# Where TensorE makes the products with the values in a slot of the local attention layers

## The chip, the cores and the metric

The kernel runs on one core of a Trainium2 chip. The metric is the device time of one launch in microseconds; less is better. Everything is computed in single precision.

## What is computed

The reference is a stack of four blocks on 4 sequences of 256 tokens of 128 features. Each block is a cross attention and a feed forward part, both gated. The change touches only the feed forward part of the first block. That one is itself a transformer of six layers with local attention:

```python
for i in range(DEPTH):                      # DEPTH = 6
    x = attn_layer(shift_tokens(x), Wqkv[i], q_scale[i], k_scale[i], Wo[i]) + x
    x = ffn_layer(shift_tokens(x), ln_g[i], ln_b[i], W1[i], b1[i], W2[i], b2[i]) + x
```

`attn_layer` makes queries, keys and values for 16 heads of 64 features, normalises queries and keys to length one, rotates them by tables, and lets each window of 32 queries look at its own 32 keys and the 32 before them, with a softmax over those 64. `ffn_layer` is a layer norm, a product with W1 (128 x 682), a split into a hidden half `a` and a gate half, `a * gelu(gate)`, and a product with W2.

## The kernel before, in words

Every engine (TensorE, VectorE, ScalarE, GpSimd and SyncE for the DMAs) has its own queue, written out by hand; semaphores hold them together. Before and after the local layers come other stages, which the change leaves alone. The local layers are `pe_local`, `act_local`, `dve_local`, `pool_local` and one for SyncE.

The work of the local layers is cut into 96 units: 6 layers x 4 sequences x 2 tiles of 128 tokens x 2 halves of 8 heads. `for slot in range(LOCAL_SLOTS)` runs over 108 slots, and a unit passes through several slots in a pipeline: in slot u its queries, keys and values are made (L616, L636, L625), in slot u + 2 queries (L645) and keys (L653) are turned, in slot u + 3 the scores are made (L675), in slot u + 5 the softmax weights are turned (L686) and multiplied with the values (L702), in slot u + 6 the output product is made (L717). "Turned" is a transpose by TensorE against the identity, four blocks of 128x128.

The feed forward part belongs to a sequence and layer, that is to four units, and its pieces hang on every fourth slot: the centring product of its layer norm (L234) and the variance product (L244) in one slot, two slots later the first gate products (L557, L558) and the third (L566), one slot later the hidden products (L574, L575 and, separately, the last one, L583), one slot later the product with W2 (L592). I call these, by what stands in them, the variance slot, the gate slot, the open slot, and again the variance slot of the next; the slot that has none is plain. In each cycle of four slots there is a variance slot, a plain slot, a gate slot and an open slot, in that order. (L557 and L558 stand ahead of L636 and so appear in the timeline at the end of the stretch that begins with the plain slot's scores.)

The buffers in PSUM are single: queries, keys, values, turned queries and keys (the bank TB), turned weights (PB) and feed forward (FB) have one bank each. So most products wait for the copy out of their bank. The waits that matter here:

- L702 waits for ScalarE's copy of the turned weights (L842), for the value windows that SyncE moves, and for the copy of the values (L804).
- L645 waits for ScalarE's copy of the turned keys (L820), L717 for the copy of the weighted values (L850).
- L244 waits for ScalarE's squares (L239, `ln_squared`).
- L566 waits for ScalarE's copies of both gate products (L866 and L867, `gate01_kept`), L574 for that of the third (L873).

ScalarE's own order in a slot is: squares of the queries (L790), exponentials (L835), the third gate's copy (L873), turned queries (L811), values (L804), squares of the keys (L797), turned weights (L842), gate copies (L866, L867), squares for the layer norm (L239), gelu with its two table loads (L880 to L882), turned keys (L820), weighted values (L850), norms (L826 to L830). VectorE's L953 adds the mask to the scores (`masked`), and L583 waits for it.

Of the kernel before, what the change touches and what calls it, by code (L numbers as in the profile page):

```python
# [195 lines left out]
UNITS = DEPTH * B * LAYER_UNITS  # L196
TURN, SCORE, SOFT, VALUE, OUT = 2, 3, 4, 5, 6
CENTRE, SQUARE, VAR, RSTD, NORM, SCALE = 10, 10, 10, 11, 11, 11
GATES, KEEP, GATE2, KEEP2, GELU, OPEN, MIX = 12, 12, 12, 13, 13, 13, 13
LAST, HIDE, MERGE, RENEW = 13, 14, 14, 15  # L200
# [12 lines left out]
def ended(slot, lag):  # L213
    lb, rest = divmod(slot - lag, LAYER_UNITS)
    return lb if rest == 0 and 0 <= lb < DEPTH * B else None
# [6 lines left out]
def home_of(lb):  # L222
    return lb // B + 1, lb % B
# [9 lines left out]
def pe_ln_centre(e, s, m, bank, src):  # L233
    e.matmul(bank[:, 0:N], m.centre, src, start=True, stop=True, skip_group_check=True).then_inc(s["ln_centred"], 1)  # L234
# [27 lines left out]
def pe_ln4(e, s, m, first, bufs):  # L262
    for b in range(B):
        pe_ln_var(e, s, m, first + b, ln_views(bufs[b]), m.bank[2 * b])
# [277 lines left out]
def pe_centre(e, s, m, lb):  # L542
    e.wait_ge(s["y_added"], 4 * lb + 4)
    if lb:
        e.wait_ge(s["a01_done"], lb)
    pe_ln_centre(e, s, m, m.bank[FB], m.zs[lb % B])
# [6 lines left out]
def pe_gates(e, s, m, lb):  # L553
    stage, b = home_of(lb)
    w1 = m.W(stage, "W1")
    e.wait_ge(s["xn_scaled"], lb + 1)
    e.matmul(m.bank[FB][:, 0:N], w1[:, FF:FF + P], m.xn[b], start=True, stop=True, skip_group_check=True)  # L557
    e.matmul(m.bank[FB][:, N:2 * N], w1[:, FF + P:FF + 2 * P], m.xn[b], start=True, stop=True,  # L558
             skip_group_check=True).then_inc(s["gate01_made"], 1)
# [19 lines left out]
def pe_last_hidden(e, s, m, lb, scored):  # L579
    stage, b = home_of(lb)  # L580
    rows = FFC[2][1]
    e.wait_ge(s["masked"], scored)
    e.matmul(m.bank[S1][0:rows, N:2 * N], m.W(stage, "W1")[:, 2 * P:FF], m.xn[b], start=True, stop=True,  # L583
             skip_group_check=True).then_inc(s["a2_made"], 1)
# [12 lines left out]
def windows_loaded(u):  # L597
    even, odd = (16 * 2 * n for n in (4, 5))
    return sum(odd if unit_of(v)[3] else even for v in range(u % 2, u + 1, 2))


def live(u):
    return 0 <= u < UNITS


def pe_query(e, s, m, u):
    lb, stage, b, t, half = unit_of(u)
    if t == 0 and half == 0:
        e.wait_ge(s["z_ready"], max(lb + 1, B))
        if b == 0 and stage % 2:  # L610
            e.wait_ge(s["slot1_loaded"], loaded(stage))
        if b == 0 and stage % 2 == 0:
            e.wait_ge(s["slot0_loaded"], loaded(stage))
    if u:
        e.wait_ge(s["q_products"], u)
    e.matmul(m.bank[QB], m.zs[b][:, t * P:(t + 1) * P], m.W(stage, "Wqkv")[:, half * BANK:(half + 1) * BANK], start=True,  # L616
             stop=True, skip_group_check=True).then_inc(s["q_made"], 1)


def pe_key(e, s, m, u):  # L620
    lb, stage, b, t, half = unit_of(u)
    at = INNER + half * BANK
    if u:
        e.wait_ge(s["k_products"], u)
    e.matmul(m.bank[KB], m.zs[b][:, t * P:(t + 1) * P], m.W(stage, "Wqkv")[:, at:at + BANK], start=True,  # L625
             stop=True, skip_group_check=True).then_inc(s["k_made"], 1)


def pe_value(e, s, m, u):
    lb, stage, b, t, half = unit_of(u)  # L630
    at = 2 * INNER + half * BANK
    if 0 < u <= VALUE:
        e.wait_ge(s["v_kept"], u)
    if u > VALUE:
        e.wait_ge(s["o_kept"], u - VALUE)
    e.matmul(m.bank[VB], m.zs[b][:, t * P:(t + 1) * P], m.W(stage, "Wqkv")[:, at:at + BANK], start=True,  # L636
             stop=True, skip_group_check=True).then_inc(s["v_made"], 1)


def pe_turn_query(e, s, m, u):  # L640
    e.wait_ge(s["q_rotated"], u + 1)
    if u:
        e.wait_ge(s["k_kept"], u)
    for r in range(UP):
        made = e.transpose(m.bank[TB][:, r * P:(r + 1) * P], m.rot_q[u % ROTS][:, r * P:(r + 1) * P], m.ident)  # L645
    made.then_inc(s["q_turned"], 1)


def pe_turn_key(e, s, m, u):
    e.wait_ge(s["k_rotated"], u + 1)  # L650
    e.wait_ge(s["q_kept"], u + 1)
    for r in range(UP):
        made = e.transpose(m.bank[TB][:, r * P:(r + 1) * P], m.rot_k[u % ROTS][:, r * P:(r + 1) * P], m.ident)  # L653
    made.then_inc(s["k_turned"], 1)
# [35 lines left out]
def pe_weighted(e, s, m, u):  # L690
    v, pT = m.v64[u % 6].rearrange("p (i k d) -> p i k d", i=4, k=UP), m.pT[u % 2]
    e.wait_ge(s["p_kept"], u + 1)
    e.wait_ge(s["v64_odd"] if u % 2 else s["v64_even"], windows_loaded(u))
    e.wait_ge(s["v_kept"], min(u + VALUE + 1, UNITS))
    for c in range(2):
        for i in range(4):
            for y in range(2):
                k = 2 * c + y
                at, to = k * P + i * WINDOW, c * P + i * WINDOW
                for x in range(2):  # L700
                    rows = slice(x * DH, (x + 1) * DH)
                    made = e.matmul(m.bank[PB if x else VB][y * DH:(y + 1) * DH, to:to + WINDOW], v[rows, i, k, :],  # L702
                                    pT[rows, at:at + WINDOW], start=True, stop=True, skip_group_check=True)
    made.then_inc(s["o_made"], 1)


def pe_out(e, s, m, u):
    lb, stage, b, t, half = unit_of(u)
    wo, oT = m.W(stage, "Wo"), m.oT[u % 2]
    e.wait_ge(s["o_kept"], u + 1)  # L710
    if u + OUT - SCORE > UNITS:
        e.wait_ge(s["y_added"], u)
    else:
        e.wait_ge(s["masked"], u + OUT - SCORE)
    for k in range(UP):
        c = half * UP + k
        made = e.matmul(m.bank[S0][:, N:N + P], wo[:, c * D:(c + 1) * D], oT[:, k * P:(k + 1) * P], start=(k == 0),  # L717
                        stop=(k == UP - 1), skip_group_check=True)
    made.then_inc(s["y_made"], 1)
# [10 lines left out]
def pe_local(e, s, m):  # L730
    e.wait_ge(s["x_done"], B)
    for b in range(B):
        pe_ln_centre(e, s, m, m.bank[2 * b], m.x[b])
    pe_ln4(e, s, m, B, m.ln_first)
    for slot in range(LOCAL_SLOTS):
        if live(slot):
            pe_query(e, s, m, slot)
        if live(slot - TURN):
            pe_turn_query(e, s, m, slot - TURN)
        if live(slot - OUT):  # L740
            pe_out(e, s, m, slot - OUT)
        if ended(slot, GATES) is not None:
            pe_gates(e, s, m, ended(slot, GATES))
        if live(slot):
            pe_value(e, s, m, slot)
            pe_key(e, s, m, slot)
        if ended(slot, CENTRE) is not None:
            pe_centre(e, s, m, ended(slot, CENTRE))
        if slot == UNITS + 1:
            e.wait_ge(s["k_products"], UNITS)  # L750
        if slot == UNITS + CENTRE - 4:
            pe_idle(e, m, KB, 2)
        if live(slot - VALUE):
            pe_turn_weights(e, s, m, slot - VALUE)
        if live(slot - SCORE):
            pe_scores(e, s, m, slot - SCORE)
        if live(slot - VALUE):
            pe_weighted(e, s, m, slot - VALUE)
        if ended(slot, VAR) is not None:
            pe_var(e, s, m, ended(slot, VAR))  # L760
        if slot == UNITS + VAR - 4:
            pe_idle(e, m, KB, 8)
        if ended(slot, OPEN) is not None:
            pe_hidden(e, s, m, ended(slot, OPEN))
        if ended(slot, LAST) is not None:
            pe_last_hidden(e, s, m, ended(slot, LAST), min(slot - SCORE + 1, UNITS))
        if slot == UNITS + GATE2 - 4:
            pe_idle(e, m, KB, 3)
        if ended(slot, GATE2) is not None:
            pe_last_gate(e, s, m, ended(slot, GATE2))  # L770
        if slot == UNITS + GATE2 - 4:
            pe_idle(e, m, KB, 2)
        if live(slot - TURN):
            pe_turn_key(e, s, m, slot - TURN)
        if UNITS < slot < UNITS + VALUE:
            pe_idle(e, m, KB, 4)
        if slot == UNITS + MERGE - 4:
            for b in range(B - 1):
                e.wait_ge(s["ffn_added"], b + 1)
                pe_ln_centre(e, s, m, m.bank[2 * b], m.x[b])  # L780
            pe_idle(e, m, KB, 3)
        if ended(slot, MERGE) is not None:
            pe_ffn_out(e, s, m, ended(slot, MERGE), min(slot - SCORE + 1, UNITS))
# [1405 lines left out]
```

## Time and profile before

| | us |
|---|---|
| median of 3 runs | 1386.46 |
| lowest and highest run | 1381.38, 1390.13 |
| the profiled execution | 1376.86 |
| its span | 1375.0 |
| TensorE busy | 1260.2 (92%) |
| VectorE busy | 975.7 (71%) |
| ScalarE busy | 933.4 (68%) |
| GpSimd busy | 741.9 (54%) |

The span runs from the first to the last instruction of the profiled execution; the run's own time is 1.9 us longer. All rows below are from this one execution. The local layers take from about 190 to 1055 us of it. A row of TensorE's products has two times: when the group starts, and how long it is busy, of which the end is modelled. How long a step holds TensorE's queue is therefore read from the start of one row to the start of the next.

### The profile page before, as it was taken

Reading aid. Unit: us, or ns where it says so; the run is one execution under the profiler, and the core shown is the slowest. Engines: PE = TensorE matmul, PEld = TensorE weight load, DVE = VectorE, ACT = ScalarE, POOL = GpSimd, SP = SyncE. Lnnn points to the kernel's source line nnn. Section 1 sums busy time; section 2 is a strip of 40 time slices with the busy share of each in tenths; the row PEclk is TensorE's granted clock in tenths of the full one; section 3 lists DMA queues with packets and bytes.
Section 4 is the critical chain, followed back from the end, with each engine's and each line's share of the span. In section 5 each row is a group of like instructions: output and inputs, shape, how many; then the busy total and the mean of one; then the engine's idle time right before and its main releaser. Section 6 shows DMA issues by size and latency. Waiting matters only on the chain. (4 is left out here: it accounts for less than half of the span.)

```text
span 1375.0 us, 45266 instructions
## 1 busy us (share of the span) xinstructions
PE 1260.2 (92%) x18136; PEld 910.2 (66%) x18136; DVE 975.7 (71%) x2481; ACT 933.4 (68%) x2297; POOL 741.9 (54%) x749
## 2 busy tenths in 40 slices
PE   6999977999999999999999999999887998998767
PEld 5777635676776776667766776667676767775444
DVE  3666657887888888888877888888834545554666
ACT  5777745676777777777776777777655656654771
POOL 3444447887878887788877877878720001003000
PEclk9999999999999999999999999999999999999799
DMA  4000032222225222522242225222302000000000
GB/s 198 1 2 1 1 114 69 68 62 55 62 62 143 60 63 60 142 59 63 65 139 54 63 61 143 58 61 66 92 3 100 0 1 28 1 0 1 1 1 16
DMA packets 68320, 76.97 MB, mean 56 GB/s; under 512 B 14864, under 2 KB 62992, under 8 KB 67600
## 3 DMA queue, kind: packets, MB, share of 16 engines
q1 hardware_dynamic: 68112, 74.07, 20.2%
q8 instruction: 145, 2.38, 0.8%
q14 instruction: 63, 0.52, 0.1%
HBM read 26.31 MB, written 0.52 MB: 20 GB/s over the span
## 5 line engine op out<-in xcount | busy, mean ns | idle before, releaser
L1072 POOL TENSOR_TENSOR arena<-arena,small 128x512 f32<-128x512 f32 x96 | 100.1, 1043 | 154.1 <-DVE small L955 154.1
L820 ACT ACTIVATE arena<-banks 128x512 f32<-128x512 f32 x96 | 57.4, 598 | 149.8 <-PE banks L653 149.5
L931 DVE TENSOR_TENSOR arena<-banks,rotary 128x512 f32<-128x512 f32 x192 | 131.6, 686 | 29.3 <-ACT arena L790 17.4
L1047 POOL TENSOR_TENSOR arena<-arena 128x512 f32<-128x512 f32 x96 | 122.6, 1277 | 38.2 <-DVE arena L933 38.2
L702 PE MATMUL banks<-arena 64*64 64x32 f32 x6144 | 113.5, 222 | 18.2 <-issue 11.1
L1052 POOL TENSOR_TENSOR arena<-arena 128x512 f32<-128x512 f32 x96 | 122.5, 1276 | 0.4 <-DVE arena L933 0.4
L702 PEld LDWEIGHTS banks<-arena 64*64 64x64 f32 x6144 | 101.2, 136 | 29.8 <-issue 11.6
L503 POOL TENSOR_TENSOR arena<-arena,small 128x512 f32<-128x512 f32 x64 | 66.5, 1040 | 88.2 <-DVE small L437 88.2
L616 PE MATMUL banks<-slot,z 128*128 128x512 f32 x192 | 101.5, 611 | 7.1 <-DVE arena L933 3.6
L717 PE MATMUL banks<-arena,slot 128*128 128x128 f32 x768 | 104.2, 279 | 0.2 <-DVE arena L953 0.2
L1059 POOL TENSOR_TENSOR arena<-arena,small 128x512 f32<-128x512 f32 x96 | 100.4, 1046 | 2.3 <-ACT small L830 2.3
L1078 POOL TENSOR_TENSOR arena<-arena,small 128x512 f32<-128x512 f32 x96 | 100.1, 1042 | 0.9 <-DVE small L963 0.9
L1066 POOL TENSOR_TENSOR arena<-arena,small 128x512 f32<-128x512 f32 x96 | 100.0, 1042 | 0.0
L636 PE MATMUL banks<-slot,z 128*128 128x512 f32 x192 | 98.6, 595 | 0.0
L625 PE MATMUL banks<-slot,z 128*128 128x512 f32 x192 | 98.1, 593 | 0.0
L717 PEld LDWEIGHTS banks<-arena,slot 128*128 128x128 f32 x768 | 93.6, 192 | 1.0 <-ACT arena L850 0.4
L645 PEld LDWEIGHTS banks<-constants,arena 128*128 128x128 f32 x384 | 43.1, 143 | 72.6 <-issue 71.7
L383 ACT ACTIVATE arena<-arena,small 128x256 f32<-128x256 f32 x128 | 63.7, 500 | 39.8 <-DVE small L466 39.8
L972 DVE TENSOR_TENSOR z<-z,banks 64x128 f32<-64x128 f32 x96 | 26.6, 277 | 90.3 <-PE banks L717 90.2
L675 PE MATMUL banks<-arena 64*32 64x64 f32 x6144 | 83.4, 225 | 1.0 <-issue 0.5
L686 PEld LDWEIGHTS banks<-constants,arena 128*128 128x128 f32 x384 | 47.7, 142 | 50.1 <-issue 30.8
L675 PEld LDWEIGHTS banks<-arena 64*32 64x32 f32 x6144 | 68.1, 106 | 18.5 <-issue 18.5
(310 smaller groups left out, 3371.2 us busy)
## 6 DMA issues: line engine op xcount, KB each, us to landing
arena<-arena SPq DMA_DIRECT2D x576, 64.0 KB, 2.0
slot<-in_pack_dram SPq DMA_DIRECT2D x28, 339.5 KB
arena<-arena SPq DMA_DIRECT2D x288, 32.0 KB, 1.8
slot<-in_pack_dram SPq DMA_DIRECT2D x2, 2713.5 KB
slot<-in_pack_dram SPq DMA_DIRECT2D x1, 3333.0 KB
slot<-in_pack_dram SPq DMA_DIRECT2D x1, 2316.5 KB
slot<-in_pack_dram SPq DMA_DIRECT2D x4, 337.0 KB
slot<-in_pack_dram SPq DMA_DIRECT2D x7, 158.0 KB
```

Source lines behind the costliest of these rows:

```text
L616: e.matmul(m.bank[QB], m.zs[b][:, t * P:(t + 1) * P], m.W(stage, "Wqkv")[:, half * BANK:(half + 1) * BANK], start=True, stop=True, skip_gr ...
L636: e.matmul(m.bank[VB], m.zs[b][:, t * P:(t + 1) * P], m.W(stage, "Wqkv")[:, at:at + BANK], start=True, stop=True, skip_group_check=True).t ...
L675: made = e.matmul(m.bank[S0 + z][i * WINDOW:(i + 1) * WINDOW, r * SPAN:(r + 1) * SPAN], qT[rows, r, i * WINDOW:(i + 1) * WINDOW], kT[rows, ...
L702: made = e.matmul(m.bank[PB if x else VB][y * DH:(y + 1) * DH, to:to + WINDOW], v[rows, i, k, :], pT[rows, at:at + WINDOW], start=True, st ...
L717: made = e.matmul(m.bank[S0][:, N:N + P], wo[:, c * D:(c + 1) * D], oT[:, k * P:(k + 1) * P], start=(k == 0), stop=(k == UP - 1), skip_gro ...
L931: e.tensor_tensor(rot, made, cos, ALU.mult)
L1047: e.tensor_tensor(m.rot_q[u % ROTS], m.rot_q[u % ROTS], m.sin_q[u % 2], ALU.add).then_inc(s["q_added"], 1)
L1052: e.tensor_tensor(m.rot_k[u % ROTS], m.rot_k[u % ROTS], m.sin_k[u % 2], ALU.add).then_inc(s["k_added"], 1)
L1059: e.tensor_tensor(q, q, stretch(m.local_small[u % 4][:, 0:UH], DH), ALU.mult).then_inc(s["q_rotated"], 1)
L1066: e.tensor_tensor(k, k, stretch(m.local_small[u % 4][:, UH:2 * UH], DH), ALU.mult).then_inc(s["k_rotated"], 1)
L1072: e.tensor_tensor(p, p, stretch(m.local_small[u % 4][:, 16:24], SPAN), ALU.subtract).then_inc(s["lowered"], 1)
L1078: e.tensor_tensor(p, p, stretch(m.local_small[u % 4][:, 32:40], SPAN), ALU.mult).then_inc(s["normalised"], 1)
```

## The change

In `pe_local`, two blocks move. The products with the values (`pe_weighted`, L702) stood right behind the scores; now they stand behind the variance product, the hidden products, the third gate product and the turned keys. The last hidden product (`pe_last_hidden`, L583) goes with them and stands behind them. No other engine's order changes, and the products and waits themselves are the same.

```diff
         if live(slot - SCORE):
             pe_scores(e, s, m, slot - SCORE)
-        if live(slot - VALUE):
-            pe_weighted(e, s, m, slot - VALUE)
         if ended(slot, VAR) is not None:
             pe_var(e, s, m, ended(slot, VAR))
...
         if ended(slot, OPEN) is not None:
             pe_hidden(e, s, m, ended(slot, OPEN))
-        if ended(slot, LAST) is not None:
-            pe_last_hidden(e, s, m, ended(slot, LAST), min(slot - SCORE + 1, UNITS))
...
         if live(slot - TURN):
             pe_turn_key(e, s, m, slot - TURN)
+        if live(slot - VALUE):
+            pe_weighted(e, s, m, slot - VALUE)
+        if ended(slot, LAST) is not None:
+            pe_last_hidden(e, s, m, ended(slot, LAST), min(slot - SCORE + 1, UNITS))
```

TensorE's queue from the scores of a gate slot on, before (L675 scores, L702 products with the values, L566 third gate product, L653 turned keys, L616 next queries):

```order
L675 MATMUL banks<-arena 32x64 [waits a2_done,masked,z_ready,y_added,k_kept]
L675 MATMUL banks<-arena 32x64 x31
L702 MATMUL banks<-arena 64x32 [waits v_kept,v64_odd,p_kept]
L702 MATMUL banks<-arena 64x32 x31
L566 MATMUL banks<-xn,slot 85x256 [waits gate01_kept]
L653 MATMUL banks<-constants,arena 128x128 [waits q_kept,k_rotated]
L653 MATMUL banks<-constants,arena 128x128 x3
L616 MATMUL banks<-slot,z 128x512 [waits q_products]
```

The same place in the changed kernel:

```order
L675 MATMUL banks<-arena 32x64 [waits a2_done,masked,z_ready,y_added,k_kept]
L675 MATMUL banks<-arena 32x64 x31
L566 MATMUL banks<-xn,slot 85x256 [waits gate01_kept]
L653 MATMUL banks<-constants,arena 128x128 [waits q_kept,k_rotated]
L653 MATMUL banks<-constants,arena 128x128 x3
L702 MATMUL banks<-arena 64x32 [waits v_kept,v64_odd,p_kept]
L702 MATMUL banks<-arena 64x32 x31
L616 MATMUL banks<-slot,z 128x512 [waits q_products]
```

L566, with its wait for `gate01_kept`, now stands directly behind the scores, and the turned keys and the products with the values are queued behind it.

In an open slot of the changed kernel TensorE's queue reads (L574, L575 and L583 are the hidden products):

```order
L675 MATMUL banks<-arena 32x64 x31
L574 MATMUL banks<-xn,slot 128x256 [waits gate2_kept]
L575 MATMUL banks<-xn,slot 128x256
L653 MATMUL banks<-constants,arena 128x128 [waits q_kept,k_rotated]
L653 MATMUL banks<-constants,arena 128x128 x3
L702 MATMUL banks<-arena 64x32 [waits v_kept,v64_even,p_kept]
L702 MATMUL banks<-arena 64x32 x31
L583 MATMUL banks<-xn,slot 85x256 [waits masked]
```

Before, L702 stood ahead of L574, and L583 ahead of L653.

## Rows read from the trace of the kernel before

**Rows 1.** The page, section 1: busy time, share of the span and instructions.

```profile
PE 1260.2 (92%) x18136; PEld 910.2 (66%) x18136; DVE 975.7 (71%) x2481; ACT 933.4 (68%) x2297; POOL 741.9 (54%) x749
```

**Rows 2.** Busy time by stretch: length, PE, PEld, DVE, ACT, POOL, PEclk, DMA.

```profile
742.00:775.50 33.50, 33.05 (x661) 23.98 (x667) 28.58 (x64) 25.52 (x56) 26.84 (x26) 1.00 0.26 61
719.00:731.00 12.00, 8.96 (x156) 6.17 (x155) 5.95 (x12) 6.52 (x16) 11.07 (x15) 0.86 0.21 50
```

**Rows 3.** TensorE's waits: line, releaser, us in total, times, longest.

```profile
PE banks L702 <- issue: 11.1, 13, 2.2
...
PE banks L702 <- ACT arena L842: 6.8, 21, 0.7
PE banks L645 <- ACT arena L820: 6.6, 18, 0.8
```

**Rows 4.** Timeline of a plain slot, TensorE: start, busy, line, operation.

```profile
750.24 0.60 PE L686 MATMUL banks<-constants,arena 128*128 128x128 f32 x4
750.77 0.86 PE L675 MATMUL banks<-arena 64*32 64x64 f32 x64
751.58 1.14 PE L702 MATMUL banks<-arena 64*64 64x32 f32 x64
752.64 0.66 PE L653 MATMUL banks<-constants,arena 128*128 128x128 f32 x4
753.13 1.02 PE L616 MATMUL banks<-slot,z 128*128 128x512 f32 x2
754.08 0.63 PE L645 MATMUL banks<-constants,arena 128*128 128x128 f32 x4
754.54 1.09 PE L717 MATMUL banks<-arena,slot 128*128 128x128 f32 x8
```

**Rows 5.** Timeline of a gate slot, TensorE and ScalarE.

```profile
758.59 0.93 PE L675 MATMUL banks<-arena 64*32 64x64 f32 x64
...
760.51 0.66 PE L566 MATMUL banks<-xn,slot 128*85 128x256 f32 x2
...
759.58 0.49 ACT L867 ACTIVATE arena<-banks,slot 128x256 f32<-128x256 f32 x1
```

**Rows 6.** Timeline of a variance slot, TensorE and ScalarE.

```profile
775.34 0.86 PE L675 MATMUL banks<-arena 64*32 64x64 f32 x64
...
777.19 0.70 PE L244 MATMUL banks<-arena,constants 128*128 128x256 f32 x2
777.73 0.60 PE L653 MATMUL banks<-constants,arena 128*128 128x128 f32 x4
...
779.47 1.02 PE L616 MATMUL banks<-slot,z 128*128 128x512 f32 x2
780.33 0.60 PE L645 MATMUL banks<-constants,arena 128*128 128x128 f32 x4
780.76 1.06 PE L717 MATMUL banks<-arena,slot 128*128 128x128 f32 x8
...
775.94 0.38 ACT L239 ACTIVATE arena<-banks 128x256 f32<-128x256 f32 x1
```

**Rows 7.** Timeline of an open slot, TensorE and ScalarE.

```profile
766.03 0.86 PE L675 MATMUL banks<-arena 64*32 64x64 f32 x64
767.01 1.14 PE L702 MATMUL banks<-arena 64*64 64x32 f32 x64
...
771.26 0.63 PE L645 MATMUL banks<-constants,arena 128*128 128x128 f32 x4 [0.32 <-ACT arena L820]
...
766.36 0.60 ACT L842 ACTIVATE arena<-banks 128x512 f32<-128x512 f32 x1
...
770.52 0.60 ACT L820 ACTIVATE arena<-banks 128x512 f32<-128x512 f32 x1
```

**Rows 8.** Timeline of TensorE in the stretch from 725.6.

```profile
725.66 0.43 PE L702 MATMUL banks<-arena 64*64 64x32 f32 x14 [1.91 <-issue]
...
726.52 1.03 PE L653 MATMUL banks<-constants,arena 128*128 128x128 f32 x4
```

## The prediction

> **What bounds the kernel now.** I read the page's busy shares first, then busy time by stretch, then the list of waits, and last the timeline of one cycle of four slots. The page gives TensorE 92% of the span, 21 points more than the next engine [rows 1]. In the local layers it is tighter: of the 33.5 us from 742 to 775.5 TensorE is busy for 33.05, at the full granted clock of 2.4 GHz, while VectorE has 28.58, GpSimd 26.84 and ScalarE 25.52 [rows 2]. So in the stage that the change touches, a slot lasts as long as its products do, and anything that makes TensorE's queue stand is paid in full. The list of waits shows how little it stands today: on ScalarE's copy of the turned weights 6.8 us, on its copy of the keys 6.6 us, and 11.1 us before the products with the values for which the profile names no releaser [rows 3]. These three are all that the move could give back by way of waits.
>
> The timeline shows four kinds of slot, which repeat (start to start on TensorE). A plain slot: scores 0.81, products with the values 1.06, keys turned 0.49 [rows 4]. A gate slot has L566 behind the products with the values, a variance slot has L244 there, an open slot has the hidden products L574 and L575. There are 24 of each kind; near the end of the stage one or two lack their scores, so I count 23 gate slots, 23 variance slots, 22 open ones and 24 plain ones.
>
> **The change part by part.** Nothing is added or removed. TensorE's products with the values (64 in the trace, 1.06 us) move behind everything that used to stand after them up to the turned keys. All other engines keep their order.
>
> 1. *Gate slot.* L566 waits until ScalarE has copied both gate banks. ScalarE does this behind its copy of the turned weights, and that one starts only when the weights are turned, at about the time at which the scores start. In the rows the scores start at 758.59 and L867 ends at 759.58 + 0.49 = 760.07, 1.48 us later. Today the scores and the products with the values lie over this, and L566 starts 1.92 us after the scores, at 760.51, unhindered [rows 5]. After the change only the scores cover it (0.81 us undisturbed, rows 4). Behind L566 stand the turned keys and the products with the values, so all of it is late. The signal takes 0.05 to 0.14 us: L645 starts at 771.26 after L820's end at 770.52 + 0.60 = 771.12 gives the upper end, L702's start at 767.01 after L842's end at 766.36 + 0.60 = 766.96 the lower [rows 7]. Wait: 1.48 + 0.05 to 0.14 - 0.81 = 0.72 to 0.81 us; I take 0.77, the middle. 23 x 0.77 = +17.7 us.
>
> 2. *Variance slot.* L244 waits for the squares, L239, also queued behind the copy of the weights. It ends at 775.94 + 0.38 = 776.32, 0.98 us after the scores start (775.34); L244 today starts at 777.19 [rows 6]. After: 0.98 + 0.05 to 0.14 - 0.80 = 0.23 to 0.32, I take 0.28. 23 x 0.28 = +6.4 us.
>
> 3. *Open slot.* Here the products with the values start 0.98 us after the scores (766.03 to 767.01) instead of 0.81, since ScalarE is late with the weights, and at the end L645 waits for L820, which follows two table loads and the gelu [rows 7]. After the change the hidden products cover the first wait. The second is ScalarE's own chain, which starts with its copy of the weights; TensorE waits for its end whatever it does in between. With TensorE later after the gate slot, that copy should no longer be late, so the end comes about 0.2 us earlier after the scores' start. 22 x 0.2 = -4.4 us. Extra cost on TensorE between the two waits is hidden here by the second.
>
> 4. *Keys copied earlier.* In plain and gate slots the keys are turned 1.07 us earlier, so ScalarE's copy of them lands well before L645 needs it. Today L616 to L645 is 0.95, L645 to L717 0.46 [rows 4]; in the variance slot, where both copies land long before, the same steps take 0.86 and 0.43 [rows 6]. I read the difference as weight loads that can't go ahead because their signal comes at the last moment. Gain 0.12, and 0.03 at L717 for the same reason, 0.15 in all: 47 x 0.15 = -7.0 us. The bounds are 0 and this.
>
> 5. *Changes of tiling.* Scores and products with the values use parts of the array (64*32 and 64*64), everything else the whole. Today they stand together. After the change the whole-array work lies between them. Going in: four turns before the scores take 750.24 to 750.77, 0.53 us, where four like them with whole-array work behind take 0.43 [rows 4, 6], so 0.10. Coming out: L244 behind the products with the values takes 0.54 (777.19 to 777.73) for as many columns, so up to 0.11 [rows 6]; L653 in the plain slot takes 0.49, so 0.06 [rows 4]. What the step from 64*32 to 64*64 costs today is inside the scores' 0.81 and goes away. No row shows scores followed by whole-array work under load. Bounds for the net: 0, if the step that goes cost as much as both that come, and 0.21, if it cost nothing. I take 0.15, nearest to the going-in row plus a half of the coming-out one. It is paid in plain, gate and variance slots: 70 x 0.15 = +10.5 us.
> The Trainium skill (TensorEngine Tiling, section Key Properties) says that changing the tiling mode, not merely the tile, drains the engine. This speaks against the change, and the 0.10 us in front of the scores agrees with it. Counted by that rule there are three changes of mode per slot today and four afterwards; with one more at 0.10 the term would be 7 us instead of 10.5.
>
> 6. *The rest.* Of the 6.8 us of waits on the weights' copy [rows 3], the open slots of term 3 make up some 17 x 0.2 = 3.4. The others stand early in the stage and at its end; half of them should go: -1.8 us. GpSimd's table slots, where L686 waits, should wait slightly less as VectorE and GpSimd get ahead: -1. The last hidden product (L583) moves behind the products with the values; its wait is on the mask, which is then older, so nothing. The keys' turning needs a rotated key and a free bank, both ready a whole slot earlier: nothing. SyncE's queue is untouched.
>
> Sum: 17.7 + 6.4 - 4.4 - 7.0 + 10.5 - 1.8 - 1 = +20.4 us. Against the profiled execution, 1376.86 us (its span 1375.0), that is 1397. The profiled one lies 0.7% under the median of the runs, so on the median, 1386.46, I set 1407, 1.5% slower.
>
> **The rivals.**
> *A: the waits come, the tiling is free.* If the step from 64*32 to 64*64 costs today what two changes cost later, term 5 is 0, and with signals at 0.05 terms 1 and 2 are 16.6 + 5.3. Sum about +8: 1394. For it: the scores, with weight loads of 32 columns, take 0.81 and part of that may be the step to 64*64. Against: the 0.81 are spread over 64 products, 13 ns each, less than the 17 ns each of the products with the values, so there is little room in them for a change.
> *B: the products with the values were the ones that waited.* The 11.1 us without a releaser before them could be the transfers of the value windows, or signals that come late. They would start 0.49 us or more later [rows 4], and all of 11.1 + 6.8 + 6.6 us [rows 3] plus the 7.0 of term 4 would go, 31.5 us, against 24.1 of terms 1 and 2 with free tiling: -7, 1379, below before. It decides if the holes are covered in full. For it: 13 such holes, all at this one step. Against: of the holes, the one shown lies 14 products before the end of the 64, not ahead of them [rows 8], and a later start would not help that; the 6.6 is mostly ScalarE's chain of term 3.
> *C: the clock.* Where TensorE had stood for some 2 us the granted clock fell to 1.2 GHz: behind a hole of 1.91 us in L702, L653's four turns are busy for 1.03 us instead of 0.66 [rows 8, 4]. From 719 to 731 the mean clock is 0.86 [rows 2], so half speed held for 12 x 0.14 / 0.5 = 3.4 us, which costs up to 1.7. If the new wait in each gate slot brought one fall, 23 x 1.7 = +39 on top: 1447. Against: isolated holes of under 1 us are common here and the clock stays at full.
>
> **How the numbers follow.** A measurement of this kernel can tell about 1% from no change, 13.9 us; that is above 1400. Forecast 0.73 (1398 to 1424), A 0.14, B 0.05, C 0.08. The upper end of the forecast: waits 0.81 and 0.32 (26), tiling 0.21 in every one of 92 slots (19.3), no gain from term 4, the others as above (-7.2), gives +38: 1424. The lower end is A's: 1394, and a little noise. Range 1394 to 1425; it leaves out B and C. Slower by over 1%: most of the forecast, and C, 0.79. Within 1%: A, most of B and the forecast's low edge, 0.18. Faster: 0.03.
>
> **What would show it.** In the profile after: a wait of TensorE at L566 on ScalarE's L867, some 23 times 0.7 to 0.8 us, and at L244 on L239, 23 times about 0.3; no waits of L702 on L842; the step from scores to L653 of about 0.81 and from L653 to L702 of about 0.53; L616 to L645 of 0.86 in plain slots; open slots about 0.2 us shorter. A cycle of four slots should take about 34.0 to 34.2 us rather than 33.1. I am wrong in kind if L566 does not wait, or if the cycle is not longer; I am wrong in size if the step from L653 to L702 and the one behind it cost over 0.2 us together, or nothing.

## The result, and the profile after

The changed kernel takes 1396.0 us in the median of 15 runs, against 1385.9 for the kernel before. The ratio of the means, without the changed kernel's three longest runs, which count as slow, is 1.0064, 95% interval 1.0033 to 1.0095: slower, by 8.9 us (the medians lie 10.1 us apart). I had forecast +20.4 us. The sign is right and the measured time lies in my range, but the size is off: I called it slower by over 1%, and it is within 1%.

The page shows TensorE no less busy in share, with the same 36,272 products and weight loads:

```profile
span 1393.5 us, 45266 instructions
...
PE 1277.6 (92%) x18136; PEld 912.4 (65%) x18136; DVE 977.1 (70%) x2481; ACT 947.1 (68%) x2297; POOL 742.3 (53%) x749
```

The waits of TensorE after the change, those that answer to [rows 3] and the two new ones (line, releaser, us in total, times, longest):

```profile
PE banks L566 <- ACT arena L867: 16.3, 23, 1.4
...
PE banks L645 <- ACT arena L820: 3.9, 21, 0.2
PE banks L702 <- issue: 3.8, 6, 1.1
...
PE banks L244 <- ACT arena L239: 1.9, 11, 0.2
PE banks L702 <- ACT arena L842: 0.7, 1, 0.7
```

The two new waits are there, 23 times at L566, as forecast. But so is something that I had only given to a rival: the holes in L702 without a releaser fell from 11.1 to 3.8 us.

The timeline of the changed kernel, TensorE in a plain slot, answers to [rows 4]:

```profile
753.25 0.60 PE L686 MATMUL banks<-constants,arena 128*128 128x128 f32 x4
753.78 0.86 PE L675 MATMUL banks<-arena 64*32 64x64 f32 x64
754.57 0.66 PE L653 MATMUL banks<-constants,arena 128*128 128x128 f32 x4
755.16 1.14 PE L702 MATMUL banks<-arena 64*64 64x32 f32 x64
756.22 1.12 PE L616 MATMUL banks<-slot,z 128*128 128x512 f32 x2
757.18 0.60 PE L645 MATMUL banks<-constants,arena 128*128 128x128 f32 x4
757.62 1.06 PE L717 MATMUL banks<-arena,slot 128*128 128x128 f32 x8
```

From the scores to L717 it takes 3.84 us, before 754.54 - 750.77 = 3.77. Gate slot (TensorE, then ScalarE), which answers to [rows 5], and the scores of the open slot behind it:

```profile
761.63 0.86 PE L675 MATMUL banks<-arena 64*32 64x64 f32 x64
763.17 0.66 PE L566 MATMUL banks<-xn,slot 128*85 128x256 f32 x2 [0.68 <-ACT arena L867]
...
769.80 0.86 PE L675 MATMUL banks<-arena 64*32 64x64 f32 x64
...
762.63 0.49 ACT L867 ACTIVATE arena<-banks,slot 128x256 f32<-128x256 f32 x1
```

L867 ends at 763.12, 1.49 us after the scores' start, and L566 starts 0.05 us later: 1.54 instead of 0.81. Variance slot, which answers to [rows 6]:

```profile
744.78 0.86 PE L675 MATMUL banks<-arena 64*32 64x64 f32 x64
745.81 0.70 PE L244 MATMUL banks<-arena,constants 128*128 128x256 f32 x2 [0.17 <-ACT arena L239]
```

L244 starts 1.03 us after the scores. And the end of the cycle: the next variance slot's scores start at 778.93.

```profile
778.93 0.29 PE L675 MATMUL banks<-arena 64*32 64x64 f32 x8
```

So the steady cycle of four slots takes 778.93 - 744.78 = 34.15 us. Before it was 775.34 [rows 6] minus 742.20, that is 33.14. I had forecast 34.0 to 34.2. Slot by slot (medians of the steps from scores to scores, 22 or more of each kind): plain 7.82 to 7.85, gate 7.40 to 8.17, open 9.37 to 9.13, variance 8.58 to 9.00. The steady state is what I computed. What I missed lies between the steady cycles.

### The profile page after: what moved, and what is told of

It is laid out like the page before. It is cut to its first block and busy times, and to the rows that moved or that the text cites. A ratio compares the mean times of both kernels' runs of the same rounds, so it can differ in the third digit from the quotient of the medians.

```text
span 1393.5 us, 45266 instructions
## 1 busy us (share of the span) xinstructions
PE 1277.6 (92%) x18136; PEld 912.4 (65%) x18136; DVE 977.1 (70%) x2481; ACT 947.1 (68%) x2297; POOL 742.3 (53%) x749
## 3 DMA queue, kind: packets, MB, share of 16 engines
q8 instruction: 145, 2.38, 0.8%
## 5 line engine op out<-in xcount | busy, mean ns | idle before, releaser
L1072 POOL TENSOR_TENSOR arena<-arena,small 128x512 f32<-128x512 f32 x96 | 100.2, 1044 | 169.9 <-DVE small L955 169.9
L1047 POOL TENSOR_TENSOR arena<-arena 128x512 f32<-128x512 f32 x96 | 122.5, 1276 | 27.2 <-DVE arena L933 27.1
L702 PE MATMUL banks<-arena 64*64 64x32 f32 x6144 | 111.8, 221 | 4.5 <-issue 3.8
L702 PEld LDWEIGHTS banks<-arena 64*64 64x64 f32 x6144 | 100.4, 135 | 21.8 <-issue 20.1
L616 PE MATMUL banks<-slot,z 128*128 128x512 f32 x192 | 104.3, 625 | 6.9 <-DVE z L1021 3.4
L820 ACT ACTIVATE arena<-banks 128x512 f32<-128x512 f32 x96 | 57.4, 598 | 71.3 <-PE banks L653 71.1
L717 PE MATMUL banks<-arena,slot 128*128 128x128 f32 x768 | 103.2, 278 | 1.0 <-DVE arena L953 1.0
L1078 POOL TENSOR_TENSOR arena<-arena,small 128x512 f32<-128x512 f32 x96 | 100.2, 1044 | 0.9 <-DVE small L963 0.9
L636 PE MATMUL banks<-slot,z 128*128 128x512 f32 x192 | 100.4, 605 | 0.0
L625 PE MATMUL banks<-slot,z 128*128 128x512 f32 x192 | 100.0, 603 | 0.0
L717 PEld LDWEIGHTS banks<-arena,slot 128*128 128x128 f32 x768 | 94.1, 193 | 1.5 <-ACT arena L850 1.2
L850 ACT ACTIVATE arena<-banks 128x512 f32<-128x512 f32 x96 | 57.2, 596 | 46.5 <-PE banks L702 46.5
L645 PEld LDWEIGHTS banks<-constants,arena 128*128 128x128 f32 x384 | 46.7, 142 | 59.8 <-issue 58.9
L675 PE MATMUL banks<-arena 64*32 64x64 f32 x6144 | 83.3, 224 | 0.6 <-DVE arena L996 0.5
L675 PEld LDWEIGHTS banks<-arena 64*32 64x32 f32 x6144 | 67.9, 105 | 18.1 <-issue 18.1
```

What stands on the lines that cost most here:

```text
L675: made = e.matmul(m.bank[S0 + z][i * WINDOW:(i + 1) * WINDOW, r * SPAN:(r + 1) * SPAN], qT[rows, r, i * WINDOW:(i + 1) * WINDOW], kT[rows, ...
L1047: e.tensor_tensor(m.rot_q[u % ROTS], m.rot_q[u % ROTS], m.sin_q[u % 2], ALU.add).then_inc(s["q_added"], 1)
L1072: e.tensor_tensor(p, p, stretch(m.local_small[u % 4][:, 16:24], SPAN), ALU.subtract).then_inc(s["lowered"], 1)
L1078: e.tensor_tensor(p, p, stretch(m.local_small[u % 4][:, 32:40], SPAN), ALU.mult).then_inc(s["normalised"], 1)
```

## Where the expected loss went

From the scores of the fifth slot that has any to those of the 93rd there are 88 slots, 22 cycles. They start at 239.04 and 988.38 before, 237.74 and 994.42 after. The time between is 749.3 and 756.7 us, so the local layers lost 7.4 us, close to the 8.9 of the timed runs, though 22 cycles of about 1.0 us more should have cost 21.6. Subtract 22 times the cycle (sum of the four medians, 33.17 and 34.15): 19.6 us lay outside the regular cycle before and 5.4 after. The holes in and right behind L702 (its step to the next row, less 1.07 us) add up to 17.9 us in 16 slots before (17.3 in a first count, which the expectations below use) and 7.0 in 10 after.

Within the 88 slots the 14.2 us that went are three things. L702's steps, over their median, fell from 14.4 to 4.6 us: these are the holes. The scores' steps, at whose end L702 waits for late weights in some early slots, fell from 2.6 us to 0.1. And before there were two stretches at the lower level of the clock (1.2 GHz), each right behind a hole, from 323.8 and from 726.5, with some 3 us of longer steps in them; after there was none. The three make 15.4 us, and small changes of other steps, the other way, take back the rest.

The profiled executions themselves differ by 18.5 us, which is more than the timed runs. The rest is behind the local layers, in a stage that the change leaves alone. The same stretch of the last cross attention (from the first L1481 on), before and after, busy time by stretch as in [rows 2]:

```profile
1262.00:1327.00 65.00, 46.36 (x473) 27.46 (x473) 40.84 (x59) 55.69 (x238) 11.98 (x14) 0.87 0.00 1
```

```profile
1268.70:1343.50 74.80, 55.36 (x470) 29.45 (x472) 40.50 (x59) 56.72 (x240) 11.66 (x13) 0.65 0.00 1
```

Nearly the same work took 9.8 us longer at a mean granted clock of 0.65 instead of 0.87. This stage, from the first L1481 to the end, takes 111 to 115 us in five of the 13 profiled executions and 122 to 126 in the other eight, whatever the order of the local layers, and it spreads the runs of every kernel: the profiled execution of before, 0.7% under its median, was one of the quicker draws. A single profile against another single profile says nothing here about the last 12 us; I therefore use the local layers' own time in what follows.

**Theories.** F: the holes are TensorE's code arriving late. Each of the 64 products of L675 and L702 is recorded with a weight load, so scores and values together are 256 instructions in 1.87 us. V (rival B of the prediction): L702 waited for its value windows, or other late inputs, and now starts later. N: chance, the profile of before merely had more holes.

## The experiments

The first four kernels ran on one chip. Each is the kernel before with some lines of `pe_local` in another place, unless said otherwise; the ratios are against the kernel before.

**Only the turned keys between.**

```diff
         if live(slot - SCORE):
             pe_scores(e, s, m, slot - SCORE)
+        if live(slot - TURN):
+            pe_turn_key(e, s, m, slot - TURN)
         if live(slot - VALUE):
             pe_weighted(e, s, m, slot - VALUE)
...
-        if live(slot - TURN):
-            pe_turn_key(e, s, m, slot - TURN)
```

> From the kernel before, only the turned keys move, between the scores and the products with the values; the variance, hidden and gate products stay behind the values. Theory F (the holes in L702 are TensorE's code arriving late, because 128 products and 128 weight loads follow each other without a gap; 0.5 us of slower work between them lets it catch up): no wait at L566 or L244, the steady cycle of four slots 33.1 to 33.3 us (before 33.14, changed kernel 34.15), holes over the regular 1.07 us of L702 at most 8 us in sum (before 17.3 in 16 slots), time ratio to before about 0.992. Theory N (the holes are chance, the profile of before just had more of them): holes about 15 us, ratio 1.00 to 1.002. Theory V (L702 waited for its value windows and starts later now): as F.

Measured: 0.995 (0.991 to 0.999). The cycle is 33.32 us, a little over the expectation. Local layers 742.4 us, 6.9 less than before, of which 9.4 outside the cycle (before 19.6). Holes still in 17 slots but smaller, 11.6 us in sum, over the 8 that I allowed. The profile's wait:

```profile
PE banks L702 <- issue: 6.6, 9, 1.3
```

The split alone, without the two waits, gains. It does not tell F from V.

**The turned keys ahead of the scores.** The diff is the same, with the two added lines ahead of `pe_scores`.

> From the kernel before, only the turned keys move, ahead of the scores. The products with the values start 0.5 us later after their inputs, but still stand right behind the scores. F: the holes stay, 12 to 20 us in sum and mostly in the last third of L702's 64 products; steady cycle 32.7 to 33.0 us because L645 and L717 get their copies earlier and no change of tiling is added; ratio about 0.994. V: the holes go (under 5 us) as in the changed kernel, ratio about 0.985. N: holes anywhere from 5 to 17.

Measured: 1.0071 (1.0034 to 1.0108), cycle 33.24 us (over the 32.7 to 33.0 that I expected), holes in 22 slots with 31.8 us, all of them inside L702:

```profile
PE banks L702 <- issue: 26.3, 20, 2.5
```

The products with the values start later after their inputs, as in the changed kernel, and the holes do not go, they grow. V is out. F expected them to stay, but not to grow, and so my 0.994 was wrong. The rows of two of them (x45 and x19, x32 and x32 are the parts of one group of 64 before and behind a hole):

```profile
735.58 0.89 PE L702 MATMUL banks<-arena 64*64 64x32 f32 x45
737.57 0.53 PE L702 MATMUL banks<-arena 64*64 64x32 f32 x19 [1.11 <-issue]
...
770.21 0.67 PE L702 MATMUL banks<-arena 64*64 64x32 f32 x32
771.44 0.67 PE L702 MATMUL banks<-arena 64*64 64x32 f32 x32 [0.56 <-issue]
```

From one hole to the next is a cycle of four slots with 638 products (four times 154, and 22 of the feed forward part), and 19 - 32 = 13 fewer: 625 products, 1250 with their weight loads, 5 times 250. Counted so over the whole stage, the distances between the 22 holes of 0.1 us and more, in units of 250 records, are 5, 5, 5, 5, 4, 5, 4, 5, 14, 9, 5, 4, 5, 5, 4, 5, 4, 14, 5, 5 and 1, each within 0.05. In the kernel before they are 10, 9, 9, 14, 5, 9, 5, 4, 5, 9, 5, 14, 9 and 5 in the same way, and only the first of the 16 holes is off, by 0.07. That is not chance, so N is out too. The number has a counterpart on the page. Section 3 lists a queue of instruction packets:

```profile
q8 instruction: 145, 2.38, 0.8%
```

2.38 MB in 145 packets are 16.4 KB each, and 36,272 recorded instructions of TensorE over 145 are 250.

The trace also has the time of each of these packets, and it settles F directly. In the hole of [rows 8] the packet ran from 723.27 to 724.15 and L702 went on at 725.66; in the first one above it ran from 735.08 to 736.20 and L702 went on at 737.57. In all 13 profiled executions there are 125 places in the local layers at which two products of one L702 start over 0.3 us apart. In every one of them the second starts 1.2 to 1.6 us after the end of an instruction packet, though packets come only every 7 us or so. Inputs that land at their own times would not line up so.

**The two waits, without the keys between.**

```diff
         if live(slot - SCORE):
             pe_scores(e, s, m, slot - SCORE)
+        if ended(slot, VAR) is not None:
+            pe_var(e, s, m, ended(slot, VAR))
+        if ended(slot, GATE2) is not None:
+            pe_last_gate(e, s, m, ended(slot, GATE2))
         if live(slot - VALUE):
             pe_weighted(e, s, m, slot - VALUE)
```

(Both are taken out of their old places behind the values.)

> From the kernel before, only the variance and the third gate product move between scores and values; keys and hidden products stay behind the values. The waits of L566 (0.68) and L244 (0.24) come in full, and the scores and values are parted in two of four slots. Steady cycle 34.0 to 34.2 us. F: holes about half, 6 to 11 us, all of them in plain and open slots; ratio 1.010. N and V: holes about as before and in every kind of slot (N), ratio 1.015.

Measured: 1.0124 (1.0067 to 1.018), cycle 34.20. The holes fell to 7.4 us in 8 slots, at the low end of what F said: six in plain and open slots, two in gate slots, whose bursts were parted. The local layers take 758.4 us, 9.1 more than before; the timed ratio is higher than that, and why stays open.

**From the changed kernel, the third gate product back behind the values.**

```diff
-        if ended(slot, GATE2) is not None:
-            pe_last_gate(e, s, m, ended(slot, GATE2))
...
         if live(slot - VALUE):
             pe_weighted(e, s, m, slot - VALUE)
+        if ended(slot, GATE2) is not None:
+            pe_last_gate(e, s, m, ended(slot, GATE2))
```

> From the changed kernel, only the third gate product goes back behind the products with the values. If the wait at L566 is paid in full there, the gate slot falls from 8.17 to about 7.45 us, the steady cycle from 34.15 to about 33.45, and 23 slots bring 16 us: ratio to before about 0.996 where holes stay as few as in the changed kernel (7 us), by F and V; by N about 1.002. If the wait at L566 costs less than it shows, because what comes after it catches up, the cycle stays above 33.8.

Measured: 1.0005 (0.9959 to 1.0051), cycle 33.61, local layers 747.2. The cycle is 0.16 over the expectation. The gate slot fell to 7.38 us as expected, but the open slot rose from 9.13 to 9.38: without the wait in the gate slot ScalarE is late again in the open one, and the wait of L645 on L820, 3.9 us in the changed kernel, is 9.7 here. The wait at L566 is 0.68 us long and costs 34.15 - 33.61 = 0.54 net.

**Half of the products with the values.** The kernel with the keys ahead, and in `pe_weighted`:

```diff
-            for y in range(2):
+            for y in range(1):
```

> As the run with the keys ahead of the scores (holes of 31 us in sum, 22 of them), but only half of the products with the values are made (the half with y = 0; the other rows of those banks are left as they are), so the burst is 64 + 32 products instead of 64 + 64. F (a piece of code of some 250 recorded instructions is used up faster than the next arrives): the piece now spans at least 0.5 us of slower work beside the burst, so the holes fall to under 10 us; the slot is 0.53 us shorter beside that. N or a cause in the products with the values themselves: about half of the holes in number stay, with the same mean of 1.4 us.

Measured in one run: 1360.2 us. The holes are gone, one of 0.35 us is left. One thing I had wrong, and it makes the test better: the slot did not get shorter. The 32 products take as long as the 64:

```profile
741.81 0.86 PE L675 MATMUL banks<-arena 64*32 64x64 f32 x64
742.60 1.12 PE L702 MATMUL banks<-arena 64*64 64x32 f32 x32
743.65 1.12 PE L616 MATMUL banks<-slot,z 128*128 128x512 f32 x2
```

1.05 us against 1.06 [rows 4]; the two halves run side by side in the array. The cycle is 33.14, with 33.24 for the kernel with all products. So the same array time, with a quarter of the burst's instructions gone, loses 31 us of holes. The local layers take 735.5 instead of 758.4 us, 23 less and not 31, since another wait grew meanwhile: that of L645 on L820 went from 7.5 to 16.5 us. And the packets:

```profile
span 1358.4 us, 39122 instructions
...
q8 instruction: 121, 1.98, 0.6%
```

45,266 - 39,122 = 6144 instructions fewer, 24 packets fewer: 256 instructions in each.

**Windows moved once only.** The kernel with the keys ahead; SyncE moves the value windows of the first six units only, and the waits for them end there. Later units are multiplied with old windows.

```diff
-        for x in range(2):
+        for x in range(2 if u < 6 else 0):
             cols = slice(x * N, (x + 1) * N)
             dst = m.v64[u % 6][x * DH:(x + 1) * DH, :]
```

> As the run with the keys ahead of the scores, but the value windows are moved for the first six units only; later units multiply with those old windows. The burst of 128 products is whole. If the transfers of the windows delay the code's packets or are themselves what is waited for (V, or F with contention): holes fall from 31 us to under 10. F without contention: the holes stay, 20 to 31 us, at whole multiples of about 250 recorded instructions from each other.

Measured in one run: 1380.5 us, holes 30.0 us in 23 slots.

```profile
PE banks L702 <- issue: 24.3, 22, 2.5
...
q1 hardware_dynamic: 11856, 29.72, 6.4%
```

The transfers fell from 74 to 30 MB and the holes stayed. Two of them again lie with 19 and 32 products left in L702, like those of the kernel that moves all windows: the place is set by the count of instructions.

```profile
729.19 0.54 PE L702 MATMUL banks<-arena 64*64 64x32 f32 x19 [0.86 <-issue]
...
763.05 0.67 PE L702 MATMUL banks<-arena 64*64 64x32 f32 x32 [0.55 <-issue]
```

So neither waiting for windows nor their traffic makes the holes.

**Hidden products and keys between,** variance and gate product behind (all operations of the kernel before; the moved calls are taken out of their old places).

```diff
         if live(slot - SCORE):
             pe_scores(e, s, m, slot - SCORE)
+        if ended(slot, OPEN) is not None:
+            pe_hidden(e, s, m, ended(slot, OPEN))
+        if live(slot - TURN):
+            pe_turn_key(e, s, m, slot - TURN)
         if live(slot - VALUE):
             pe_weighted(e, s, m, slot - VALUE)
+        if ended(slot, LAST) is not None:
+            pe_last_hidden(e, s, m, ended(slot, LAST), min(slot - SCORE + 1, UNITS))
```

> All operations of the kernel before. Between scores and values stand the turned keys in every slot and, in open slots, the two hidden products, which need no copy that comes late; variance and gate product stay behind the values. Steady cycle 33.2 to 33.4 us (as with the keys alone, 33.32), holes 6 to 11 us. F: ratio to before 0.993 to 0.996.

Measured: 0.9998 (0.9963 to 1.0033), above the expectation, with a cycle of 33.33, holes of 6.5 us and local layers of 742.0 us. By these it should have gained as much as with the keys alone, so I ran both again (below).

**The key projection between as well.** L625 and the turned keys stand between scores and values, and ScalarE squares the keys behind its copy of the weights.

```diff
             pe_scores(e, s, m, slot - SCORE)
+        if live(slot):
+            pe_key(e, s, m, slot)
+        if live(slot - TURN):
+            pe_turn_key(e, s, m, slot - TURN)
```

> All operations of the kernel before. Between scores and values stand the slot's key projection (0.86 us, few instructions) and the turned keys (0.53); ScalarE copies the turned weights ahead of squaring the keys. F: 256 instructions at the burst now last at least 3.2 us instead of 1.9, so the holes go almost wholly, under 3 us, and if VectorE bears that its keys come 1.3 us later, the ratio is about 0.985. If VectorE does not (it then shows as TensorE waiting for the mask, the rotated keys or the output sum), the cycle grows over 33.5 and the ratio is about 1.00, with the holes gone all the same.

Measured: 1.073 (1.0684 to 1.0777), the second branch and much worse than I thought. I read the waits so: VectorE gets its keys late, the mask behind them, and through GpSimd the softmax comes back to TensorE late (two lines more than before in this file, so L1074 is L1072, and L1080 is L1078):

```profile
POOL arena L1074 <- DVE small L957: 264.2, 96, 8.3
...
PEld banks L686 <- POOL arena L1080: 108.0, 71, 4.0
```

Before, these two were 154.1 us and, for L686's products, 8.9 (here 61.9). The cycle is 37.67 us. The holes did not go under 3 us: 12 are left, in 21 slots. The simple form of F, that one piece of code must last longer than the fetch of the next, does not give that.

The packets' times say more. In the 125 places above, L702 goes on 2.2 to 3.1 us after its packet starts. When that packet started, 0 to 257 recorded instructions were left before the hole, most often 60 to 250. So a hole is what is missing when the instructions left last less than these 2.2 to 3.1 us; how long the whole piece of 250 lasted does not decide, it was 1.7 to 10.6 us. With the keys ahead of the scores the packets of the holes started with fewer instructions left than in the kernel before (median 114 against 215), which makes longer holes. What sets the time at which a packet starts, and so why it starts late there, stays open.

**ScalarE's order.** The changed kernel, with this in `act_local`:

```diff
-        if live(slot - VALUE):
-            act_weights(e, s, m, slot - VALUE)
         if ended(slot, KEEP) is not None:
             act_gates(e, s, m, ended(slot, KEEP))
         if ended(slot, SQUARE) is not None:
             act_ln_start(e, s, m, ended(slot, SQUARE))
+        if live(slot - VALUE):
+            act_weights(e, s, m, slot - VALUE)
```

> The changed kernel, with ScalarE's copies of the two gate products and its squares for the layer norm ahead of its copy of the turned weights instead of behind it. If the waits of L566 and L244 come from that place in ScalarE's queue and nothing else, both go (16.3 and 1.9 us): gate slot 8.17 to about 7.45, variance slot 9.00 to about 8.75, open slot back to about 9.38, steady cycle 33.4; holes stay near those of the changed kernel, 5 to 9 us by F; ratio to before 0.993 to 0.997. If the gate products themselves come late, the waits stay.

Measured: 0.997 (0.9934 to 1.0005), cycle 33.42, local layers 743.0, holes 5.7 us.

```profile
PE banks L566 <- ACT arena L867: 3.7, 16, 0.7
```

The wait at L244 is gone, that at L566 fell from 16.3 to 3.7 us. What is left comes from ScalarE's squares of the keys (L797), which stand ahead of both copies and can start only when L625 is done: in one gate slot L625's step ends at 754.43, L797 starts at 754.63, and L867 ends at 755.96, 1.00 us after the scores' start (1.49 in the changed kernel). So the two new waits were, but for this rest, the place in ScalarE's queue, as terms 1 and 2 of the prediction said. Two slots did not come out as expected: the gate slot takes 7.69 us, not 7.45, and the open slot stayed at 9.13 instead of going back to 9.38. The two misses cancel in the cycle. Against the changed kernel this one is 13.7 us quicker in the local layers (756.7 to 743.0).

**The two best ones again,** on the chip of the last.

> The kernel with only the turned keys between scores and values, once more, beside the two others on one chip: the first time its ratio was 0.995 (0.991 to 0.999). By F and its local layers (s5 to s92 742 us against 749), 0.992 to 0.997.

> The kernel with hidden products and turned keys between, once more: first 0.9998 (0.996 to 1.003), though its local layers take the same 742 us as with the keys alone. If the difference between the two was only the clock of the stages behind the local layers, both come out alike now, 0.992 to 0.998.

Measured: keys alone 0.9969 (0.9935 to 1.0004), hidden and keys 0.9986 (0.9956 to 1.0016). Local layers 742.2 and 741.8 us, holes 10.0 and 7.0. In the local layers, where they differ, they are equal. For the whole time the runs on record say more, since each has its mean granted clock over the whole execution, and the time falls with it in every kernel: by 8.8 us for each 0.01, by one line through all of them (a few far longer ones aside), around which they scatter by 2.0 us. My estimate from that line, at one mean clock of 0.965 (1 is the full clock) and against the kernel before on the same chip, is: keys between 5.9 and 3.8 us shorter, hidden products and keys 3.2 and 3.8, ScalarE's order 4.2, each within about 1.5. So the first 0.9998 came in part from the clock, the three kernels are alike, and each is about 0.3% faster than before by this estimate; by the intervals of the ratios alone only the first 0.995 is clear of 1. They are the best found. With the two waits only, 15 us longer remain at that clock.

| kernel | ratio | cycle | local layers | outside the cycle |
|---|---|---|---|---|
| before | 1 | 33.17 | 749.3 | 19.6 |
| changed | 1.0064 | 34.15 | 756.7 | 5.4 |
| keys between | 0.995 | 33.32 | 742.4 | 9.4 |
| keys ahead | 1.0071 | 33.24 | 758.4 | 27.1 |
| two waits only | 1.0124 | 34.20 | 758.4 | 6.0 |
| gate product back | 1.0005 | 33.61 | 747.2 | 7.8 |
| half of the values | | 33.14 | 735.5 | 6.4 |
| windows once | | 33.24 | 753.6 | 22.3 |
| key projection between | 1.073 | 37.67 | 842.5 | 13.8 |
| hidden and keys | 0.9998 | 33.33 | 742.0 | 8.7 |
| changed, ScalarE's order | 0.997 | 33.42 | 743.0 | 7.8 |

(The last column is the local layers' time less 22 cycles. It also holds the table slots, in which L686 waits: four of about 1 us before.)

## Why the prediction was wrong in size

Term 1, the gate slot: right. I said 0.77 us per slot; the step is 1.54 instead of 0.81, so 0.73, and the signal took 0.05, the lower end. The kernel with ScalarE's order shows the cause. Put back, the wait gives 0.54 per cycle, net of what the open slot loses.

Term 2, the variance slot: right. 0.28 said, 1.03 - 0.79 = 0.24 found.

Term 3, the open slot: right, 0.2 said, 9.37 - 9.13 = 0.24 found. It goes when the gate slot falls to 7.38 us (the kernel with the gate product back) and stays when that is 7.69 (ScalarE's order). So a longer gate slot brings it, as I had it, but 0.3 us of it is enough.

Terms 4 and 5: right in sum. In the plain slot the keys' earlier copy and the tiling were to cancel, -0.15 and +0.15; the slot went from 7.82 to 7.85. L645 to L717 and L717's own step fell to 0.44 and 0.89 as said. L616 to L645 stayed at 0.96 where I had said 0.86, since the gain of 0.09 and the loss of 0.10 for coming out of the tiling meet in this step. The second try of the keys between shows the two apart, with the keys early in both slots: 0.96 where L616 follows L702, 0.86 where L566 stands between them.

```profile
748.06 1.12 PE L616 MATMUL banks<-slot,z 128*128 128x512 f32 x2
749.02 0.60 PE L645 MATMUL banks<-constants,arena 128*128 128x128 f32 x4
...
755.90 0.66 PE L566 MATMUL banks<-xn,slot 128*85 128x256 f32 x2
756.40 1.02 PE L616 MATMUL banks<-slot,z 128*128 128x512 f32 x2
757.26 0.60 PE L645 MATMUL banks<-constants,arena 128*128 128x128 f32 x4
```

The scores' step is 0.79 instead of 0.81, so today's change from 64*32 to 64*64 costs 0.02 at most; L653 between the two takes 0.59 instead of 0.43, and L616 behind L702 0.10 more than its 0.86, less the 0.06 that L653 paid before: 0.18 net. That is near the end of my bounds (0.21) at which the step that goes costs nothing. The Trainium skill (TensorEngine Tiling, section Key Properties) says that a change of tiling mode drains the engine. The trace agrees in so far as whole to part costs 0.10 us and part to whole 0.06 to 0.11; for part to part it shows 0.02 at most. Counted as one more change at 0.10, the term would have been about half of the 0.18 found.

Term 6 and the sum: here is the step that failed. I added the terms of the steady cycle and let nearly everything outside it stand. Term 6 gave it 2.8 us, for late weights and table slots, and the 11.1 us without a releaser [rows 3] and the slow clock behind them [rows 8] got no term at all. What lay outside the cycle was 19.6 us, and the change took 14.2 of them away, 9.8 of it as holes in L702. 22 x 0.98 - 14.2 = +7.4. Rival B had the place right and named a wrong cause, late inputs, and I dismissed it with a row that should have made me ask: a hole 14 products before the end of a group cannot be an input's, since nothing there waits. It says that the instructions themselves were late. Counting the records between two such holes, possible with the trace of before alone, would have given 250 and the instruction packets on the page. A piece of slower work between the two groups of 128 instructions was then a possible gain to be priced. That the sign of the sum came out right is no merit of the sum: the cycle's 21.6 us happened to be more than the 14.2.

Rival C, the clock, did not come: within the 88 slots the clock fell twice before and never after. Rival A had the time nearly right (1394 against 1396) by a wrong sum: its tiling was not free.

## What to carry over

A wait "issue" in the midst of a run of equal instructions is no semaphore. Count the records between such holes, and compare their ends with the times of the instruction queue's packets; if both fit, it is the code that is late, and not the inputs. Fewer instructions helped here, and so did slower work between the two dense groups, but not the same work ahead of them. And an order change is priced in two parts, the steady cycle (which rows give within a few hundredths) and what is not in the cycle. Before moving a product ahead on TensorE, look at where its copy stands in ScalarE's queue: moving that copy as well gave back 13.7 us of the local layers' time.

## What the runs showed of the hardware

- TensorE's code comes in packets of 16.4 KB, 256 instructions each (24 packets less for 6144 instructions less). TensorE stopped for 0.2 to 2.5 us inside L702, at whole multiples of 250 recorded instructions, and went on 1.2 to 1.6 us after a packet's end, 2.2 to 3.1 us after its start (125 places in 13 profiles). The holes were there with 74 and with 30 MB of other transfers (31.8 and 30.0 us).
- The 64 products of L702 (64*64, 32 columns), in four places of the array, take 1.06 us, and the 32 of them that use only one of the two column places take 1.05.
- In the rows of this kernel, going from whole-array products to 64*32 or 64*64 ones cost 0.10 us, coming back 0.06 to 0.11, changing between the two part sizes 0.02 or nothing.
- The last cross attention ran at a mean granted clock of 0.87 in one execution and 0.65 in another, with nearly the same work in it, 65 against 74.8 us. From its start to the end of the kernel there were two groups of executions, 111 to 115 and 122 to 126 us, which is a spread of about 1% of the kernel's time.
